# Row maxima of an attention kernel: five of twelve places per head pair take the queries' high part in row halves, 512 keys each

## The chip, the cores and the metric

The kernel is one program on one core of a Trainium2 chip. The metric is device time in microseconds, the median of several executions. The engines are TensorE (PE in the rows, its weight loads PEld), VectorE (DVE), ScalarE (ACT), GpSimd (POOL) and SyncE (SP), which issues most transfers.

## The reference

One layer on x of 8 sequences, 1024 tokens, width 256: causal attention with 16 heads over a latent of 64 numbers per token, a layer norm, a top-1 mixture of 32 experts with a capacity of 320 rows each, and a second layer norm.

```python
q = einsum('bld,dhk->blhk', x, Wq)
latent = einsum('bld,dc->blc', x, Wkv_down)
k = einsum('blc,chk->blhk', latent, Wk_up)
v = einsum('blc,chk->blhk', latent, Wv_up)
attn = softmax(where(mask, einsum('bqhd,bkhd->bhqk', q, k) / 8, -inf))
x = layernorm(x + einsum('bqhd,hdo->bqo', einsum('bhqk,bkhd->bqhd', attn, v), Wout))
x = layernorm(x + experts(x))        # router, capacity 320, silu(g) * u, gate
```

## The kernel before

The key and value matrices are folded into the query and output matrices, so that a head's query is 64 numbers wide and is multiplied with the latents directly. Queries and latents are split into a high and a low part, each in the rounded 32-bit type that TensorE multiplies in one pass. `q_hl[..][:, h, :]` holds 128 rows for head h: for head 0 the high part in rows 0 to 63 and the low part in rows 64 to 127, for head 1 the other way round. `lat_hi` holds the latents' high part twice, in both row halves. One matmul over 128 rows therefore multiplies a head's whole query with the latents' high part.

The main loop runs over 64 steps `gp` (8 sequences of 8 head pairs; p is the pair in its sequence) and 12 slots `t` in each, one for a block of 128 keys against 512 queries. The order on each engine is written out by hand:

- `turned_scores` (L742, L745) makes scores with keys on the partitions, for ScalarE's exponentials (L1011). The second matmul brings in the low latents and the row's maximum, which `q_max` holds as a 65th row.
- For that maximum the scores are made a second time, with queries on the partitions: `row_scores` (L717). Each call is a *unit*: a head, a block of 128 queries and up to 512 keys, into one of three PSUM banks in turn (`ROW_BANKS`). VectorE takes each unit's maximum in `row_max`: with the causal mask (L1175) where the unit ends on the diagonal, plainly (L1179) otherwise. A unit's matmul waits until the maximum of the unit three before it is done (`ROW_BEFORE`).
- `values` (L765) multiplies the exponentials with the latents, a head in each half of the array's columns, at even t for the two slots before the last two.

There are 24 units in a step, in pairs (both heads). `UNITS` lists them, and pair k is put at `PLACES[k]`: slot t, and 0 for right behind the slot's scores or 1 for the slot's end. The places (0, 0), (4, 0), (6, 0), (8, 0) and (10, 0), numbers 0, 4, 6, 8 and 10, stand right in front of value products. Step gp makes the units of step gp + 1, so 63 steps have them; step 0's own are made at the start. Widths of the pairs before, places 0 to 11: 128, 256, 384, 512, 320, 320, 512, 256, 512, 384, 512, 512 keys.

VectorE's order in slots 6 to 8 matters below: the two maxima of place 6, `copy_max` (L1190) of the transposed maxima that TensorE makes after the values (L727), `invert_rows` (L1209 four times, L1213), the two maxima of place 7, those of place 8, `invert_rows` again. Other matmul stages that follow a pair in some steps are `project_q` (L664), `turn_x` (L674), `turn_latents` (L690) and `total` (L777). L858 is a product of the setup.

Of the kernel before, what the change touches and what calls it, by code (L numbers as in the profile page):

```python
# [9 lines left out]
ACT = mybir.ActivationFunctionType  # L10
AX = mybir.AxisListType
F32 = mybir.dt.float32
# [4 lines left out]
P = 128  # L17
# [6 lines left out]
def build_layer(nc, x, Wq, Wkv, Wk_up, Wv_up, Wout, w_router, w_gate, w_up, w_down, out):  # L24
    B, L, D = x.shape
    _, H, HD = Wq.shape
    LD = Wkv.shape[1]
    E, _, F = w_gate.shape
    T = B * L
    C = int(math.ceil(1.25 * T / E))  # L30
    NT = L // P
# [3 lines left out]
    HPB = BANK // P  # L35
# [14 lines left out]
    first_query = lambda t: P * max(0, SLOT[t][1] - HPB * SLOT[t][0])  # L50
    on_diagonal = lambda t: SLOT[t][1] >= HPB * SLOT[t][0]

    UNITS = ([(h, i, 0) for i in range(HPB) for h in range(2)]
             + [(h, i, k) for i in range(HPB, NT) for k in range(2) for h in range(2)])
    NU = len(UNITS)

    unit_keys = lambda i, k: ((k * 5 * P // 2, (k + 1) * 5 * P // 2) if i == HPB
# [3 lines left out]
    PLACES = [(0, 0), (0, 1), (1, 1), (2, 1), (4, 0), (4, 1), (6, 0), (7, 0), (8, 0), (8, 1), (10, 0), (10, 1)]  # L61
# [4 lines left out]
    UNIT_ORDER = [(0, u) for u in range(2 * HPB)] + [unit for at in sorted(UNITS_AT) for unit in UNITS_AT[at]]  # L66
    UNIT = {unit: n for n, unit in enumerate(UNIT_ORDER)}
    assert len(UNIT) == PAIRS * NU == len(UNIT_ORDER)

    kept_by = lambda n: n // NSLOT * NT + sum(on_diagonal(t) for t in range(n % NSLOT + 1))  # L70
    NPROBS = 6
# [15 lines left out]
    with ExitStack() as ctx:  # L87
        def sb(name, shape, dt=F32, stack=ctx):
            return stack.enter_context(nc.sbuf_tensor(name, shape, dt))
# [10 lines left out]
        stat6 = sb("stat6", [P, 16, 6])  # L100
# [18 lines left out]
        lat_hi = [sb(f"lat_hi{i}", [P, L], F32R, attn) for i in range(2)]  # L119
        lat_lo = [sb(f"lat_lo{i}", [LD + 1, L], F32R, attn) for i in range(2)]  # L120
        lat_keys = [sb(f"lat_keys{i}", [P, NT, LD], F32, attn) for i in range(2)]
        q_hl = [sb(f"q_hl{i}", [P, 2, L], F32R, attn) for i in range(2)]
# [14 lines left out]
        x1 = sb("x1", [P, NT, W], F32, attn)  # L137
# [4 lines left out]
        alone = sb("alone", [P, 3, NT], F32, attn)  # L142
# [14 lines left out]
        x_in = [sb(f"x_in{i}", [P, NT, D], F32, attn) for i in range(2)]  # L157
# [17 lines left out]
        tail = ExitStack()  # L175
# [5 lines left out]
        NY = 5  # L181
# [1 line left out]
        ex_xT = sb("ex_xT", [P, 2, KD, 2 * C], F32, tail)  # L183
        ex_s = sb("ex_s", [P, 4, KF, C], F32, tail)
        ex_h = sb("ex_h", [P, 4, KF, C], F32, tail)
        ex_y = sb("ex_y", [P, 2, NY, D], F32, tail)
        neg_mean = sb("neg_mean", [P, 2 * NY], F32, tail)
        shift = sb("shift", [P, 2 * NY], F32, tail)
        tail.close()
# [61 lines left out]
        ex_sent = [sem(f"ex_sent{i}") for i in range(4)]  # L251
# [25 lines left out]
        for gp in range(PAIRS):  # L277
            b, p = divmod(gp, NPAIR)
# [85 lines left out]
        ex_ring = [row_ps[0], row_ps[1], value_ps, misc_ps]  # L364
# [5 lines left out]
        def _(sp):  # L370
# [23 lines left out]
            for gp in range(PAIRS):  # L394
                b, p = divmod(gp, NPAIR)
# [49 lines left out]
            sp.wait_ge(alone_stored, 16 * B)  # L445
            for e in range(AHEAD, E):
                g = (e - AHEAD) // 2
                sp.wait_ge(ex_sent[g % 2], 16 * NY * (g // 2 + 1))
                load_rows(e)
                load_weights(e)  # L450
            for k in range(2):
                sp.wait_ge(ex_sent[k], 16 * NY * (E // 4))

        @block.gpsimd
        def _(pool):
# [121 lines left out]
            for gp in range(PAIRS):  # L577
                b, p = divmod(gp, NPAIR)
# [42 lines left out]
            def send_back(g):  # L621
                pool.wait_ge(ex_o_ready, g + 1)
                for n in range(NY):
                    nc.gpsimd.indirect_dma_start(
                        out=out_rows, out_offset=bass.IndirectOffsetOnAxis(
                            ap=ex_x[:, g % (AHEAD // 2), n, TOKEN:W].bitcast(I32), axis=0),
                        in_=ex_y[:, g % 2, n, :], in_offset=None, bounds_check=T - 1, oob_is_err=False
                        ).then_inc(ex_sent[g % 2], 16)

            for g in range(E // 2):  # L630
                root(g)
# [3 lines left out]
        def _(pe):  # L635
# [67 lines left out]
            def row_scores(gp, u):  # L703

                h, i, k = UNITS[u]
                n = UNIT[gp, u]
                b = gp // NPAIR
                if u in (0, 2 * HPB):
                    wait_emptied(pe, ("q", gp, u // (2 * HPB)))
                    if gp % NPAIR == 0:  # L710
                        wait_emptied(pe, ("lat", b, u // (2 * HPB)))
                if n >= 2:
                    if n in ROW_BEFORE:
                        pe.wait_ge(max_done, ROW_BEFORE[n] + 1)
                k0, k1 = unit_keys(i, k)
                dst = ROW_BANKS[row_bank(n)]
                nc.tensor.matmul(dst[:, 0:k1 - k0], q_hl[gp % 2][:, h, i * P:(i + 1) * P], lat_hi[b % 2][:, k0:k1],  # L717
                                 start=True, stop=True).then_inc(rows_full, 1)

            def turn_max(gp, c):  # L720
# [119 lines left out]
            for c in range(4):  # L840
                bank = take(("wqT", c))
# [4 lines left out]
            bank = take(("wkT", 0))  # L846
# [6 lines left out]
            for kd in range(KD):  # L853
                banks = [take(("A", h, kd)) for h in range(2)]
                for j in range(NPAIR):
                    for h in range(2):
                        rows = slice(h * HD, (h + 1) * HD)
# [15 lines left out]
            bank = take(("wvT", 0))  # L873
# [4 lines left out]
            for c in range(4):  # L878
                banks = [take(("V", h, c)) for h in range(2)]
                for j in (2 * c, 2 * c + 1):  # L880
                    for h in range(2):
                        rows = slice(h * HD, (h + 1) * HD)
# [94 lines left out]
        def _(act):  # L977
# [50 lines left out]

            def pass_alone(b, i):

                act.wait_ge(x1_ready, b * 2 + i // HPB + 1)
                act.wait_ge(alone_scale, b * 2 + i // HPB + 1)
                ins = nc.scalar.activation(x_in[b % 2][:, i, :], x1[:, i, 0:D], ACT.Identity, scale=alone[:, 2, i:i + 1])
                if i == NT - 1:
                    ins.then_inc(alone_ready, 1)

# [9 lines left out]
            bank = wait_full(act, use)  # L1046
            nc.scalar.copy(wkT, bank).then_inc(free_of(use), 1)
            for kd in range(KD):
                for h in range(2):
                    bank = wait_full(act, ("A", h, kd))  # L1050
                    dst = fold_hi[:, kd, :].rearrange("p (j h c) -> p j h c", h=2, c=LD)[:, :, h, :]
# [46 lines left out]
            def normalise_out(g):  # L1098
                act.wait_ge(shift_ready, g + 1)
                for n in range(NY):  # L1100
                    k = g % 2 * NY + n
                    last = nc.scalar.activation(ex_y[:, g % 2, n, :], ex_y[:, g % 2, n, :], ACT.Identity,
                                                bias=shift[:, k:k + 1], scale=rstd[:, k:k + 1])
                last.then_inc(ex_o_ready, 1)

# [8 lines left out]
        def _(dve):  # L1114
# [265 lines left out]
            def add_to_rows(g):  # L1380

                part = slice(g % 2 * NY, (g % 2 + 1) * NY)
                if g >= 2:
                    dve.wait_ge(ex_sent[g % 2], 16 * NY * (g // 2))
                for n in range(NY):
                    bank, _ = y_use(g, n)
                    row = ex_x[:, g % (AHEAD // 2), n, :]
                    dve.wait_ge(ex_y_full, g * NY + n + 1)
                    nc.vector.scalar_tensor_tensor(ex_y[:, g % 2, n, :], ex_ring[2 + bank][:, 0:D],
                                                   row[:, GATE:TOKEN], row[:, 0:D], ALU.mult, ALU.add  # L1390
                                                   ).then_inc(ex_y_free[bank], 1)
                for n in range(NY):
                    bank, uses = y_use(g, n)
                    dve.wait_ge(ex_y_free[bank], uses + 1)
                    last = nc.vector.bn_stats(stat6[:, g % 2 * NY + n, :], ex_y[:, g % 2, n, :])
                step(last)
                settle()
                for n in range(NY):
                    last = nc.vector.bn_aggr(mean_var[:, g % 2 * NY + n, :], stat6[:, g % 2 * NY + n, :])
                last.then_inc(var_ready, 1)  # L1400
# [30 lines left out]
```

## Time and profile before

| | |
|---|---|
| median of 3 runs | 2441.88 us (2440.73 to 2442.39) |
| profiled execution, its own time | 2441.89 us |
| its span on the core | 2440.1 us |
| mean granted TensorE clock | 0.974 |
| TensorE matmuls busy | 2319.8 us, 95% |
| weight loads busy | 1509.0 us, 62% |
| VectorE | 1517.1 us, 62% |
| ScalarE | 1041.7 us, 43% |
| GpSimd | 1715.3 us, 70% |
| row units' matmuls (L717) | 1536, 512 keys in 640 of them |

The page gives each engine's busy time and the chain that ended last. The timeline gives the start and the length of single instructions. Matmuls are pipelined: a matmul of 512 columns is shown 0.40 us long, but the next starts 0.24 us after it. So what a matmul costs is read from start to start, not from its length. A line with "x2" merges two instructions in a row. Where two lines merge, the time in front covers both.

### The profile page before, as it was taken

How to read it: one execution, taken by the hardware profiler on the slowest of the kernel's cores; microseconds unless marked ns; L12 is line 12 of the kernel's file. 1: busy time of each engine (PE TensorE's matmuls, PEld its weight loads, DVE VectorE, ACT ScalarE, POOL GpSimd, SP SyncE). 2: the span in 40 equal slices, each digit the busy share in tenths (PEclk: the TensorE clock that was granted, in tenths of full speed). 3: DMA queues.
4: the chain of work that ended last, by engine and by line, in shares of the span. 5: the costliest groups of instructions: out<-in, count | busy, mean ns of one | idle time of the engine just before them, and what ended most of it. 6: DMA issues, size and time to landing. Idle time of an engine off the chain costs nothing.

```text
span 2440.1 us, 36843 instructions
## 1 busy us (share of the span) xinstructions
PE 2319.8 (95%) x11528; PEld 1509.0 (62%) x11528; DVE 1517.1 (62%) x4450; ACT 1041.7 (43%) x2048; POOL 1715.3 (70%) x1774
## 2 busy tenths in 40 slices
PE   6999999999999999999999999999999999849996
PEld 5565576556655666567655765566656665537774
DVE  4677656765576657765776567656766577225553
ACT  3454435543455445443544354534554454112222
POOL 0688767986788667975797669867886679524444
PEclk8999999999999999999999999999999999969998
DMA  3222200200011001100020002100110011234552
GB/s 89 62 65 62 62 10 19 65 24 18 14 44 49 14 14 36 53 19 14 19 73 21 10 19 61 27 18 14 44 49 14 14 33 41 67 110 150 183 184 67
DMA packets 96819, 118.97 MB, mean 49 GB/s; under 512 B 12288, under 2 KB 75782, under 8 KB 96624
## 3 DMA queue, kind: packets, MB, share of 16 engines
q1 hardware_dynamic: 89712, 99.98, 14.9%
q0 software_dynamic: 6912, 16.64, 2.0%
q8 instruction: 93, 1.52, 0.3%
q14 instruction: 102, 0.84, 0.1%
HBM read 46.91 MB, written 37.90 MB: 35 GB/s over the span
## 4 chain that ended last, share of the span: by engine, by line
PE 83%; DVE 7%; issue 4%; POOL 3%; ACT 2%; DMA 0%; SPq 0%; DVEq 0%; POOLq 0%; ACTq 0%
PE value_ps L765 20%; PE misc_ps L787 9%; PE turned_ps L742 9%; PE turned_ps L745 9%; PE misc_ps L664 8%; PE row_ps L717 7%; PE turned_ps L938 6%; PE turned_ps L717 3%; PE misc_ps L777 2%; DVE rinv L1209 1%; PE value_ps L957 1%; PE misc_ps L957 1%; POOL half_sums L516 1%; DVE masked_row L1175 1%; PE misc_ps L813 1%
## 5 line engine op out<-in xcount | busy, mean ns | idle before, releaser
L1011 ACT ACTIVATE probs<-turned_ps 128x512 f32<-128x512 f32 (+2 forms) x1280 | 647.7, 555 | 779.6 <-PE turned_ps L745 749.1
L516 POOL TENSOR_TENSOR half_sums<-half_sums,probs 128x1024 f32<-128x1024 f32 (+3 forms) x512 | 832.2, 1625 | 30.0 <-ACT probs L1011 14.1
L765 PE MATMUL value_ps<-probs,lat_keys 128*64 128x512 f32 (+3 forms) x3072 | 589.1, 505 | 2.2 <-POOL probs L491 2.2
L742 PE MATMUL turned_ps<-q_hl,lat_hi 128*128 128x512 f32 (+2 forms) x1280 | 500.2, 393 | 1.5 <-ACT fold_v L1064 1.5
L745 PE MATMUL turned_ps<-q_max,lat_lo 65*128 65x512 f32 (+2 forms) x1280 | 480.4, 375 | 1.8 <-DMA q_max<-both_rows 1.8
L491 POOL TENSOR_SCALAR_AFFINE_SELECT probs<-probs 128x256 f32<-128x256 f32 x512 | 210.6, 411 | 354.6 <-ACT probs L1011 352.0
L1175 DVE CUSTOM_DVE_ANT_0 masked_row<-row_ps,future 128x512 bf16<-128x512 f32 (+4 forms) x707 | 344.7, 508 | 136.5 <-PE row_ps L717 130.4
L765 PEld LDWEIGHTS value_ps<-probs,lat_keys 128*64 128x64 f32 x3072 | 188.2, 137 | 278.0 <-issue 211.6
L511 POOL TENSOR_TENSOR half_sums<-probs 128x768 f32<-128x768 f32 (+1 forms) x128 | 269.6, 2106 | 118.7 <-ACT probs L1011 118.6
L717 PE MATMUL row_ps<-lat_hi,q_hl 128*128 128x512 f32 (+4 forms) x1026 | 340.6, 373 | 4.9 <-DVE neg_max L1175 4.0
L717 PEld LDWEIGHTS row_ps<-lat_hi,q_hl 128*128 128x128 f32 x1026 | 189.6, 191 | 150.7 <-issue 69.7
L742 PEld LDWEIGHTS turned_ps<-q_hl,lat_hi 128*128 128x128 f32 x1280 | 243.3, 190 | 39.2 <-ACT probs L1011 10.0
L745 PEld LDWEIGHTS turned_ps<-q_max,lat_lo 65*128 65x128 f32 x1280 | 244.2, 191 | 27.7 <-DMA q_max<-both_rows 2.3
L1179 DVE TENSOR_REDUCE unit_max<-row_ps 128x1 f32<-128x512 f32 (+1 forms) x319 | 199.9, 643 | 77.0 <-PE row_ps L717 77.0
L787 PE MATMUL misc_ps<-fold_v,headsT 128*128 128x256 f32 x1008 | 232.5, 383 | 6.3 <-DVE x L1237 3.6
L787 PEld LDWEIGHTS misc_ps<-fold_v,headsT 128*128 128x128 f32 x1008 | 187.6, 190 | 47.4 <-issue 13.9
L717 PE MATMUL turned_ps<-lat_hi,q_hl 128*128 128x320 f32 x510 | 182.4, 358 | 6.5 <-DVE unit_max L1175 2.7
L523 POOL TENSOR_TENSOR headsT<-headsT,rinv_rows 128x512 f32<-128x512 f32 x128 | 165.4, 1292 | 22.7 <-DVE rinv_rows L1213 22.7
L991 ACT CAST q_hl<-misc_ps 64x512 fp32r<-64x512 f32 x125 | 72.6, 581 | 216.6 <-PE misc_ps L664 216.6
L1175 DVE CUSTOM_DVE_ANT_0 masked_row<-turned_ps,future 128x256 bf16<-128x256 f32 (+1 forms) x317 | 160.6, 507 | 3.4 <-PE turned_ps L717 1.5
L938 PE MATMUL turned_ps<-ex_xT,ex_w 128*128 128x320 f32 x512 | 145.6, 438 | 0.0
L1237 DVE TENSOR_TENSOR x<-misc_ps,x_in 128x256 f32<-128x256 f32 x64 | 27.2, 425 | 186.7 <-PE misc_ps L787 186.7
(195 smaller groups left out, 2728.2 us busy)
## 6 DMA issues: line engine op xcount, KB each, us to landing
q_max<-q_hl SPq DMA_DIRECT2D x256, 128.0 KB
slots_x<-router SPq DMA_DIRECT2D x8, 1290.0 KB, 5.9
ex_x<-slots_x SPq DMA_DIRECT2D x64, 129.0 KB, 2.3
x_in<-in_L_attn_x_bld SPq DMA_DIRECT2D x8, 1024.0 KB, 5.6
layer_out<-x_in SPq DMA_DIRECT2D x8, 1024.0 KB, 4.5
ex_w<-in_L_ffn_w_gate SPq DMA_DIRECT2D x32, 256.0 KB, 3.7
ex_w<-in_L_ffn_w_up SPq DMA_DIRECT2D x32, 256.0 KB, 3.8
ex_w<-in_L_ffn_w_down SPq DMA_DIRECT2D x32, 256.0 KB, 4.4
```

The costliest lines, as they stand in the source:

```text
L491: nc.gpsimd.affine_select(out=block, in_=block, pattern=[[0, 2], [1, P]], compare_op=ALU.is_ge, fill=0.0, base=0, channel_multiplier=-1).t ...
L511: nc.gpsimd.tensor_tensor(sums_of(gp, c)[:, :, q0:BANK], before[:, :, q0:BANK], now[:, :, q0:BANK], ALU.add).then_inc(added, 1)
L516: nc.gpsimd.tensor_tensor(total, total, now[:, :, q0:BANK], ALU.add).then_inc(added, 1)
L717: nc.tensor.matmul(dst[:, 0:k1 - k0], q_hl[gp % 2][:, h, i * P:(i + 1) * P], lat_hi[b % 2][:, k0:k1], start=True, stop=True).then_inc(rows ...
L742: nc.tensor.matmul(scores_of(n, h), lat_hi[b % 2][:, keys], q_hl[gp % 2][:, heads, cols], start=True, stop=False)
L745: nc.tensor.matmul(scores_of(n, h), lat_lo[b % 2][:, keys], q_max[:, c, heads, q0:BANK], start=False, stop=True).then_inc(turned_full, 1)
L765: mm = nc.tensor.matmul(value_ps[h * LD:(h + 1) * LD, q0:BANK], lat_keys[b % 2][:, j, :], probs[:, n % NPROBS, h, q0:BANK], start=(j == 0) ...
L787: mm = nc.tensor.matmul(bank[:, 0:D], headsT[:, (NPAIR * b + j) % NHEADS, i * P:(i + 1) * P], fold_v[:, j, :], start=(j == 0), stop=(j == ...
L938: mm = nc.tensor.matmul(turned_ps[f][:, m, 0:C], ex_w[e % AHEAD][:, m, kd, f * P:(f + 1) * P], ex_xT[:, g % 2, kd, u * C:(u + 1) * C], sta ...
L1011: nc.scalar.activation(probs[:, n % NPROBS, heads, q0:BANK], scores_of(n, h), ACT.Exp).then_inc(exp_done, 1)
L1175: nc.vector.tensor_tensor_reduce(masked_row[n % 2][:, 0:width], row[:, 0:width], future[:, BANK - width:], scale=-1.0, scalar=-MASKED, op0 ...
L1179: nc.vector.tensor_reduce(dst, row[:, 0:width], AX.X, ALU.max, negate=True).then_inc(max_done, 1)
```

## The change

`UNITS` has another order. Widths of the pairs are now 512, 128, 256, 384, 512, 320, 512, 320, 512, 256, 512, 384 keys for places 0 to 11: the same units, but all five places in front of value products now have 512 keys. In those five places a unit's matmul takes only the 64 rows of its own head's high part (`rows_of`): rows 0 to 63 for head 0, rows 64 to 127 for head 1. The queries' low part is left out of these maxima; they only shift the exponent, and the sums are made with the same shift. Step 0's own units keep 128 rows. The rest of the diff gives names to sizes (`NOUT = 2`, `x_out`) and changes no instruction.

```diff
-    UNITS = ([(h, i, 0) for i in range(HPB) for h in range(2)]
-             + [(h, i, k) for i in range(HPB, NT) for k in range(2) for h in range(2)])
+    UNITS = [(h, i, k) for i, k in ((3, 0), (0, 0), (1, 0), (2, 0), (5, 0), (4, 0), (6, 0), (4, 1), (7, 0), (5, 1), (7, 1), (6, 1))
+             for h in range(2)]
...
+    IN_ROW_HALVES = [k for k, (t, end) in enumerate(PLACES) if t % 2 == 0 and not end]
+    rows_of = lambda gp, u, h: slice(h * LD, (h + 1) * LD) if gp and u // 2 in IN_ROW_HALVES else slice(0, P)
...
-                nc.tensor.matmul(dst[:, 0:k1 - k0], q_hl[gp % 2][:, h, i * P:(i + 1) * P], lat_hi[b % 2][:, k0:k1],
+                rows = rows_of(gp, u, h)
+                nc.tensor.matmul(dst[:, 0:k1 - k0], q_hl[gp % 2][rows, h, i * P:(i + 1) * P], lat_hi[b % 2][rows, k0:k1],
                                  start=True, stop=True).then_inc(rows_full, 1)
```

## Rows read from the trace of the kernel before

**Rows 1.** Page, part 4: the chain that ended last, by engine.
```profile
PE 83%; DVE 7%; issue 4%; POOL 3%; ACT 2%; DMA 0%; SPq 0%; DVEq 0%; POOLq 0%; ACTq 0%
```
**Rows 2.** Windows, one step: length, then each engine's busy time, clock, DMA.
```profile
100.65:127.63 26.98, 26.83 (x136) 16.11 (x134) 19.55 (x59) 13.40 (x27) 22.86 (x22) 1.00 0.24 69
```
**Rows 3.** Timeline of a pair of 512 before values, and a pair after them.
```profile
1002.86 0.40 PE L745 MATMUL turned_ps<-q_max,lat_lo 65*128 65x512 f32 x1
...
1003.33 0.40 PE L717 MATMUL row_ps<-lat_hi,q_hl 128*128 128x512 f32 x1
1003.66 0.20 PEld L765 LDWEIGHTS value_ps<-probs,lat_keys 128*64 128x64 f32 x4 [0.37 <-ACT probs L1011]
...
1005.53 0.50 PE L717 MATMUL row_ps<-lat_hi,q_hl 128*128 128x512 f32 x1
1005.63 0.19 PEld L717 LDWEIGHTS turned_ps<-lat_hi,q_hl 128*128 128x128 f32 x1
1005.86 0.39 PE L717 MATMUL turned_ps<-lat_hi,q_hl 128*128 128x512 f32 x1
```
**Rows 4.** Timeline: a load of 64 rows behind a matmul over the full array.
```profile
533.25 0.40 PE L745 MATMUL turned_ps<-q_max,lat_lo 65*128 65x512 f32 x1
...
533.58 0.57 PEld L690 LDWEIGHTS misc_ps<-ident,x1T 64*128 64x128 f32 x8 [0.37 <-issue]
```
**Rows 5.** Setup product in row halves: first loads; all loads (min/median/max ns); window.
```profile
19.41 0.32 PEld L858 LDWEIGHTS turned_ps<-headsT 64*128 64x128 f32 x2 [1.45 <-ACT headsT L1047]
...
L858 PEld LDWEIGHTS turned_ps<-headsT x64: 282/330/330, 19.4 to 26.0; 64*128 64x128 f32 x64
...
19.50:26.10 6.60, 6.60 (x63) 6.60 (x64) 1.29 (x2) 1.09 (x2) 0.00 (x0) 0.50 0.01 2
```
**Rows 6.** Timeline: last score matmul and first value product around places 0, 4, 4.
```profile
92.58 0.39 PE L745 MATMUL turned_ps<-q_max,lat_lo 65*128 65x512 f32 x1
...
93.08 1.73 PE L765 MATMUL value_ps<-probs,lat_keys 128*64 128x512 f32 x8
...
100.41 0.40 PE L745 MATMUL turned_ps<-q_max,lat_lo 65*128 65x512 f32 x1
...
101.14 0.65 PE L765 MATMUL value_ps<-probs,lat_keys 128*64 128x512 f32 x2
...
236.24 0.39 PE L745 MATMUL turned_ps<-q_max,lat_lo 65*128 65x512 f32 x1
...
236.85 1.08 PE L765 MATMUL value_ps<-probs,lat_keys 128*64 128x512 f32 x4
```
**Rows 7.** Timeline, places 6 to 8: VectorE's chain and the load that waits for it.
```profile
106.60 1.29 DVE L1179 TENSOR_REDUCE unit_max<-row_ps 128x1 f32<-128x512 f32 x2 [1.15 <-PE row_ps L717]
...
107.52 0.27 PE L727 MATMUL misc_ps<-ident,neg_max 128*8 128x128 f32 x1
...
107.90 0.28 DVE L1190 CAST both_rows<-misc_ps 8x128 fp32r<-8x128 f32 x1
...
110.29 0.19 PEld L717 LDWEIGHTS turned_ps<-lat_hi,q_hl 128*128 128x128 f32 x1 [0.58 <-DVE unit_max L1175]
...
2064.89 0.19 PEld L717 LDWEIGHTS turned_ps<-lat_hi,q_hl 128*128 128x128 f32 x1 [0.58 <-DVE unit_max L1175]
```
**Rows 8.** Groups by form: one masked maximum of 256 and of 320 keys.
```profile
L1175 DVE CUSTOM_DVE_ANT_0 masked_row<-turned_ps,future 128x256 bf16<-128x256 f32 x126 | 50.8, 403 | 2.7 <-PE turned_ps L717 0.7 <-issue 0.2
...
L1175 DVE CUSTOM_DVE_ANT_0 masked_row<-turned_ps,future 128x320 bf16<-128x320 f32 x64 | 31.1, 486 | 0.0
```
**Rows 9.** Timeline: place 10 of a step with p = 6.
```profile
252.58 0.40 PE L745 MATMUL turned_ps<-q_max,lat_lo 65*128 65x512 f32 x1
...
253.53 1.94 PE L765 MATMUL value_ps<-probs,lat_keys 128*64 128x512 f32 x8
```
**Rows 10.** Timeline: a unit of 256 keys and the matmul behind it.
```profile
108.68 0.29 PE L717 MATMUL row_ps<-lat_hi,q_hl 128*128 128x256 f32 x1
108.81 0.40 PE L742 MATMUL turned_ps<-q_hl,lat_hi 128*128 128x512 f32 x1
```

More of the change, by code:

```diff
@@ L185, in build_layer @@
         ex_h = sb("ex_h", [P, 4, KF, C], F32, tail)
-        ex_y = sb("ex_y", [P, 2, NY, D], F32, tail)
+        NOUT = 2
+        ex_y = sb("ex_y", [P, NOUT, NY, D], F32, tail)
         neg_mean = sb("neg_mean", [P, 2 * NY], F32, tail)
@@ L447, in _ @@
                 g = (e - AHEAD) // 2
-                sp.wait_ge(ex_sent[g % 2], 16 * NY * (g // 2 + 1))
+                sp.wait_ge(ex_sent[g % NOUT], 16 * NY * (g // NOUT + 1))
                 load_rows(e)
                 load_weights(e)
-            for k in range(2):
-                sp.wait_ge(ex_sent[k], 16 * NY * (E // 4))
+            for k in range(NOUT):
+                sp.wait_ge(ex_sent[k], 16 * NY * (E // 2 // NOUT))
         @block.gpsimd
@@ L626, in send_back @@
                             ap=ex_x[:, g % (AHEAD // 2), n, TOKEN:W].bitcast(I32), axis=0),
-                        in_=ex_y[:, g % 2, n, :], in_offset=None, bounds_check=T - 1, oob_is_err=False
-                        ).then_inc(ex_sent[g % 2], 16)
+                        in_=ex_y[:, g % NOUT, n, :], in_offset=None, bounds_check=T - 1, oob_is_err=False
+                        ).then_inc(ex_sent[g % NOUT], 16)
             for g in range(E // 2):
@@ L1029, in pass_alone @@
             def pass_alone(b, i):
+                x_out = x_in[b % 2]
                 act.wait_ge(x1_ready, b * 2 + i // HPB + 1)
                 act.wait_ge(alone_scale, b * 2 + i // HPB + 1)
-                ins = nc.scalar.activation(x_in[b % 2][:, i, :], x1[:, i, 0:D], ACT.Identity, scale=alone[:, 2, i:i + 1])
+                ins = nc.scalar.activation(x_out[:, i, :], x1[:, i, 0:D], ACT.Identity, scale=alone[:, 2, i:i + 1])
                 if i == NT - 1:
@@ L1101, in normalise_out @@
                     k = g % 2 * NY + n
-                    last = nc.scalar.activation(ex_y[:, g % 2, n, :], ex_y[:, g % 2, n, :], ACT.Identity,
+                    last = nc.scalar.activation(ex_y[:, g % NOUT, n, :], ex_y[:, g % NOUT, n, :], ACT.Identity,
                                                 bias=shift[:, k:k + 1], scale=rstd[:, k:k + 1])
@@ L1382, in add_to_rows @@
                 part = slice(g % 2 * NY, (g % 2 + 1) * NY)
-                if g >= 2:
-                    dve.wait_ge(ex_sent[g % 2], 16 * NY * (g // 2))
+                if g >= NOUT:
+                    dve.wait_ge(ex_sent[g % NOUT], 16 * NY * (g // NOUT))
                 for n in range(NY):
@@ L1388, in add_to_rows @@
                     dve.wait_ge(ex_y_full, g * NY + n + 1)
-                    nc.vector.scalar_tensor_tensor(ex_y[:, g % 2, n, :], ex_ring[2 + bank][:, 0:D],
+                    nc.vector.scalar_tensor_tensor(ex_y[:, g % NOUT, n, :], ex_ring[2 + bank][:, 0:D],
                                                    row[:, GATE:TOKEN], row[:, 0:D], ALU.mult, ALU.add
@@ L1394, in add_to_rows @@
                     dve.wait_ge(ex_y_free[bank], uses + 1)
-                    last = nc.vector.bn_stats(stat6[:, g % 2 * NY + n, :], ex_y[:, g % 2, n, :])
+                    last = nc.vector.bn_stats(stat6[:, g % 2 * NY + n, :], ex_y[:, g % NOUT, n, :])
                 step(last)
```

## The prediction

> **What bounds the kernel now.** I read the chain first: 83% of what ended last is TensorE, 7% VectorE [rows 1]. One step shows the same: in 26.98 us TensorE's matmuls cover 26.83, VectorE works 19.6 and GpSimd 22.9 [rows 2]. GpSimd has 4 us to spare in a step, so no change of some tenths makes it the bound. What counts is when matmuls start, so the rest is read from the timeline, start to start. There a pair of 512 keys at place 10 stands like this [rows 3]: last score matmul at 1002.86, the second unit two matmuls later at 1003.33, first load of the values at 1003.66. A matmul of 512 costs 0.235 while the array goes on in the same shape. The last step is 0.33, that is 0.095 more: values use column halves, and their load is not started under the running matmul, it waits until the array is empty. After the values it is the same, and the unit's own load is open too: first unit at 1005.53, second load let in at 1005.63, second unit at 1005.86. So an open load is 0.107 (0.33 less the 0.23 of a unit). Pairs in front of values have the emptying behind them already.
>
> **A pair in row halves.** The diff hopes that the two units run side by side. The question is what stands in front of them: the array goes from 128 rows to 64. That step is in the trace [rows 4]: a load of 64 rows and 128 columns behind the same L745 starts 0.33 after it (533.25 to 533.58), in all seven steps that have one (0.318 to 0.330). So changing the row shape empties the array as changing the column shape does. I price the new pair from the last score matmul on: 0.33 until the loads start, 0.107 for the open load, then 0.23 and 0.095 until the values' load: 0.762. That holds if the second head's load and matmul go beside the first's. Row halves are in the trace once, in a setup product [rows 5]: the first two loads cover 0.32 together, where the shortest of the 64 takes 0.282, so the second starts 0.04 after the first at most; all 64 fit in about 6.6 us at the granted clock of 0.5 (1.2 GHz), a pair in 0.21. So loads lie side by side. For the matmuls the rows are weaker: 0.21 for a pair of them would also hold two in a row of 64 columns and two passes each (half of the 0.21 at that clock). I take side by side, and 0.77 for the pair: the bounds are 0.762 and 0.80 (the full 0.04 added). The bound from the other side, matmuls in a row, is 1.00.
>
> The Trainium skill, TensorEngine Tiling (Array Packing), Theoretical Speedup, says that a contraction of at most 64 gives up to twice the rate; by that alone 315 pairs (5 in each of 63 steps) would each save one unit of 0.235, 74 us in all, for 2368. The same page, Key Properties, says that a change of the tiling mode drains TensorE, and the trace agrees with this one (0.33 against 0.235).
>
> **The five places.** Before, a pair costs, from last score matmul to values: place 0 (128 keys) 0.50; place 4 (320) 0.73 where the second load waits for VectorE, 0.61 where not (p = 1, 2, 6); places 6, 8, 10 (512) 0.80 [rows 3, 6]. After, each is 0.77. So place 0 is +0.27, place 4 +0.04 (+0.15 or so for p = 1, 2, 6), the others -0.025 each. Place 4's wait goes, as place 3 now has 384 keys for VectorE instead of 512.
>
> **The other seven.** 128 keys are worth 0.058 on a matmul: 512 cost 0.235, 256 cost 0.12 [rows 3, 10]. Places 2, 3, 9 and 11 lose 128 keys in both units: 4 x 0.115 = -0.46. Place 1 goes from 256 to 128, but there a load (0.107) is longer than the matmul, so only -0.03. Place 7 goes from 256 to 320: +0.06. Together -0.43.
>
> **Where TensorE runs free** a step's sum is 0.27 + 0.04 - 0.075 - 0.43 = -0.195, or -0.085 with the dearer place 4.
>
> **The wait at place 8.** In 27 of the 63 steps (p = 4, 5, 7, those with p = 1 to 3 of the first sequence, and the last) the second unit of place 8 waits for VectorE; its load comes at 110.29 in the first of them, at 2064.89 in the last, with 0.58 idle before [rows 7]. Its bank is freed by the first maximum of place 7, and VectorE reaches that by a chain that starts with place 6: two maxima from 106.60, the copy at 107.90, four reciprocals, a transpose, the mask. What happens to the chain's start? Before, the first unit of place 6 starts 0.235 after the last score matmul and VectorE follows 0.43 behind. Now both units really start at 0.437, so VectorE begins 0.20 later, though the pair as a whole is done earlier. Of this 0.095 is absorbed: the copy at 107.90 waits for TensorE's L727 (107.52, it always comes 0.38 later), and could follow the maxima 0.095 sooner, as it does in the steps where VectorE is late. That leaves 0.105, and the mask of 320 keys instead of 256 adds 0.07 (486 against 403 ns [rows 8], a little less from start to start). So the load at place 8 comes 0.18 later than now, and nothing that TensorE saved at places 6 or 8 helps. A step with this wait: 0.27 + 0.04 - 0.025 (place 10) + 0.18 (places 6 to 8 with place 7) - 0.49 (places 1, 2, 3, 9, 11) = -0.025. Behind the waiting load stand the values of slot 8 and everything after them on TensorE; VectorE has 0.8 us idle before place 9, so the delay is not passed on twice.
>
> In steps with p = 6 VectorE is late already at place 6, so the later start costs nothing; there place 10 takes 0.95 (252.58 to 253.53) instead of 0.80 [rows 9] because it waits for place 9's masks, which shrink from 384 to 256 keys: -0.145 more, so -0.23. In steps with p = 3 the spare time before place 8 is 0.08 and shrinks to some 0.03: still free. For p = 0, 1, 2 other work stands in slot 7 and the spare time is above 0.4.
>
> **The sum.** 14 steps (p = 0, 3) x -0.195 = -2.7; 14 (p = 1, 2) x -0.085 = -1.2; 7 (p = 6) x -0.23 = -1.6; 27 x -0.025 = -0.7. Step 0 and the setup units have the same units in another order, behind VectorE there: 0, give or take 0.5. In all -6.2 us on the profiled execution's 2441.89 (span 2440.1 and 1.8 around it; the runs' median is 2441.88, the same): 2435.7, say 2436. VectorE, ScalarE and GpSimd have the same instructions; no DMA is added or moved, and SyncE's queue is untouched. The maxima of places 0 to 3 are done before TensorE transposes them in slot 6 as before.
>
> The largest unknown is the pair's 0.77. Some 256 pairs count with their length (not those of places 6 and 8 in the waiting steps): down to 0.762 is -2 us, up to 0.80 is +8. The chain's 0.18 may be 0.10 to 0.27 (nothing or everything absorbed): -2 to +2.5, and p = 3 and 6 could join with 0.15 each: +2. That gives 2431 to 2448.
>
> **Rivals.** *The loads are hidden*: if the emptying and the open load don't come, a pair costs 0.565, 0.205 less, 315 times: -65, so about 2371. The step of [rows 4] and the other six like it speak against it. Chance 5%. *The gain is eaten*: the second head trails by the full 0.04 and the chain passes all of its delay on: 2441.9 - 6.2 + 8 + 2.5 = 2446; with half of this 2441. What speaks for it is the 0.04 of [rows 5], though taken at the lower clock. This and the upper half of my own case fall within 0.2%, or 4.9 us, which is about what a measurement of this kernel can tell from no change. Chance of that band 30%. *Slower, because the halves take turns*: at each of the 315 pairs the second matmul starts only when the first is through. The second load then lies under the first matmul, so the price is 0.23, against 0.235 saved; with the emptying and the open load left over, +0.23 x 315 = +72, so about 2508. If only the loads take turns it is 0.107 x 315 = +34, so about 2470. It decides from 0.02 per pair, where the free steps' gain is gone. The setup product's loads [rows 5] speak against it for the loads, and say little on the matmuls; the four loads of column halves within 0.20 [rows 3] are the next nearest. Chance 10% for both together; 3% more for a granted clock that falls to its lower level in more stretches, as half of the array rests in ten matmuls of a step; and 4% for smaller delays above 2447.
>
> **Chances.** My case, 2431 to 2437: 48%. Faster by over 0.2% is 53% with the hidden loads; within 0.2% 30%; slower 17%. The range that leaves 2 in 10 out takes in the first two cases and not their far ends: 2427 to 2448. Most of what lies outside is above it.
>
> **What would show it.** In the changed kernel's timeline: from L745 to the units' loads 0.33 (right) or 0.24 (hidden loads); the two loads of a pair within 0.04, and the pair from score matmul to values 0.77; place 8's wait in the same 27 steps with its load 0.18 later after place 6; no wait at places 4 and 10. It is wrong if the pair takes over 0.80 (taking turns: about 1.00), if the wait at place 8 spreads to the steps with p = 0 or 2, or if the granted clock has more low stretches.

## The result

The changed kernel takes 2450.91 us (2449.33 to 2452.29, five executions) where the kernel before takes 2441.88 beside it. The ratio is 1.0040, with a 95% interval of 1.0026 to 1.0055. The change is slower by 9 us; the forecast was 2436.0, faster by 6. The profiled execution took 2450.91 us too, its span is 2449.2 us, 9.1 more than before, and the mean granted clock 0.971 for 0.974.

The page of the changed kernel, parts 1 and 4 (the second line answers [rows 1]):

```profile
PE 2323.4 (95%) x11528; PEld 1444.4 (59%) x11528; DVE 1516.3 (62%) x4450; ACT 1040.6 (42%) x2048; POOL 1712.0 (70%) x1774
...
PE 82%; DVE 6%; issue 4%; POOL 4%; ACT 3%; DMA 1%; SPq 0%; POOLq 0%; DVEq 0%; ACTq 0%
```

Weight loads lost 65 us of busy time and no other engine moved by more than 4. The shares of the chain can't tell 9 us. As in the forecast, the readings come from the timeline, start to start. The step that [rows 2] showed, in the same kind of window:

```profile
100.50:127.50 27.00, 26.90 (x136) 15.22 (x134) 19.52 (x59) 13.37 (x27) 22.81 (x22) 1.00 0.24 69
```

It takes as long as before, 27.00 and 26.98 us. The forecast for such a step, one with the wait at place 8, was 0.025 less.

**The pair is as forecast.** Timeline of the changed kernel at place 10 of the step of [rows 3], which stood there with 0.80 us from score matmul to values:

```profile
1005.61 0.39 PE L751 MATMUL turned_ps<-q_max,lat_lo 65*128 65x512 f32 x1
...
1005.93 0.49 PE L723 MATMUL turned_ps<-lat_hi,q_hl 64*128 64x512 f32 x1
1005.94 0.50 PE L723 MATMUL row_ps<-lat_hi,q_hl 64*128 64x512 f32 x1
1006.37 1.94 PE L771 MATMUL value_ps<-probs,lat_keys 128*64 128x512 f32 x8
...
1005.93 0.18 PEld L723 LDWEIGHTS turned_ps<-lat_hi,q_hl 64*128 64x128 f32 x1 [0.35 <-DVE unit_max L1182]
1005.94 0.18 PEld L723 LDWEIGHTS row_ps<-lat_hi,q_hl 64*128 64x128 f32 x1
```

0.32 to the first load, the second head 3 to 4 ns behind it, 0.43 to the values: 0.755 in all, just under the 0.762 to 0.80 of the forecast. The two heads do run side by side. They start 3 to 5 ns apart in 232 of the 315 pairs; in the other 83, nearly all at places 4, 8 and 10, the second unit's bank is not free yet.

**At place 4 TensorE still waits for a mask of place 3.** The stretch answers the second of [rows 6], which had 0.73 there; 0.77 was forecast, and it is 0.88:

```profile
98.23 0.68 DVE L1162 TENSOR_TENSOR q_hl<-misc_ps,q_hl 64x512 fp32r<-64x512 f32 x1 [0.31 <-ACT q_hl L998]
98.42 0.62 PE L723 MATMUL row_ps<-lat_hi,q_hl 128*128 128x384 f32 x2
...
98.93 0.69 DVE L1163 TENSOR_TENSOR q_hl<-misc_ps,q_hl 64x512 fp32r<-64x512 f32 x1
...
99.65 0.56 DVE L1182 CUSTOM_DVE_ANT_0 masked_row<-row_ps,future 128x384 bf16<-128x384 f32 x1
99.82 0.39 PE L751 MATMUL turned_ps<-q_max,lat_lo 65*128 65x512 f32 x1
...
100.14 0.49 PE L723 MATMUL turned_ps<-lat_hi,q_hl 64*128 64x512 f32 x1
100.27 0.50 PE L723 MATMUL row_ps<-lat_hi,q_hl 64*128 64x512 f32 x1
100.70 1.08 PE L771 MATMUL value_ps<-probs,lat_keys 128*64 128x512 f32 x4
```

The second unit starts 0.13 after the first, not 3 ns. Its bank is freed by the first mask of place 3. That mask is shorter now, but it starts at 99.65, behind the two subtractions that make the queries' low part (L1162, L1163), and those wait for ScalarE's copies. TensorE comes to place 4 earlier by what place 3 saved, and finds VectorE where it was.

**The stage bank is waited for more.** `misc_ps` is one PSUM bank that all stages but scores, units and values share. Waits of TensorE's loads, from before and then from the changed kernel: engine, tile and line, what was waited for, then total us, times, longest:

```profile
PEld misc_ps L664 <- DVE q_hl L1156: 11.8, 7, 1.7
...
PEld misc_ps L787 <- DVE x L1237: 6.0, 7, 1.0
...
PEld misc_ps L674 <- DVE q_hl L1156: 2.8, 7, 0.4
```

```profile
PEld misc_ps L669 <- DVE q_hl L1163: 12.8, 7, 1.8
...
PEld misc_ps L793 <- DVE x L1244: 8.8, 20, 1.0
...
PEld misc_ps L679 <- DVE q_hl L1163: 4.2, 7, 0.6
```

The stage behind `q_hl` in slot 3 waits 0.2 longer in each of its seven steps (2.8 to 4.2; for p = 1 and 2 other stages, L787 and L805, stand there and grow alike), and the bank that holds a projection until VectorE has added it (L1237, now L1244) is waited for 20 times instead of 7. The row of before that carries the first one was on the page of waits when I made the forecast; I did not ask what the shorter units would do to it.

**In steps with p = 3, place 11 waits too.** The second unit of place 11 takes the bank that the first maximum of place 10 frees, and VectorE comes to that maximum late, behind the low part of the queries and the tile count. The load in the fourth sequence, from before and then changed:

```profile
951.78 0.19 PEld L717 LDWEIGHTS turned_ps<-lat_hi,q_hl 128*128 128x128 f32 x1 [0.34 <-DVE unit_max L1179]
```

```profile
954.36 0.19 PEld L723 LDWEIGHTS turned_ps<-lat_hi,q_hl 128*128 128x128 f32 x1 [0.46 <-DVE unit_max L1182]
```

Slot 10 is 0.15 to 0.17 shorter for p = 0, 1 and 2; for p = 3 it is 0.01 longer.

**The changed kernel's step, class by class.** Starts of the same matmul in both traces, compared slot by slot (median of the sequences after the first, us):

| steps | forecast | measured | of it given back |
|---|---|---|---|
| 27 with the wait at place 8 | -0.025 | +0.024 | place 4 +0.15 for +0.04 |
| p = 0, 7 | -0.195 | +0.012 | place 4; slots 9 and 11 +0.06, +0.11 |
| p = 3, 7, its first slot left out | -0.195 | near 0 | place 4; slot 10 +0.16 |
| p = 1, 7 | -0.085 | +0.225 | slot 3 +0.20; slots 9 and 11 +0.06, +0.11 |
| p = 2, 7 | -0.085 | +0.095 | slot 3 +0.20; slot 11 +0.12 |
| p = 6, 7 | -0.230 | +0.381 | slot 3 +0.20; slots 9 and 11 +0.10, +0.11 |

In slots 9 and 11 it is not always the same wait: the stage bank for p = 0 and 1, ScalarE's copy of `x1T` in front of the routing product for p = 2, the next sequence's `xT_lo` and `lat_lo` from VectorE for p = 6.

27 x 0.024 + 7 x (0.012 + 0.225 + 0.095 + 0.381) = 5.6, where the forecast had -4.8 for these and -1.4 for p = 3.

**Most of the rest is clock.** Of the remaining 3.5 us some 2.5 lie in the first slot of the steps with p = 3 and the slot before it, and 1.2 in the experts' tail, where the clock is at 0.5 for 3.4 us more twice (start and step 0 are 0.6 shorter). In front of a step with p = 3 TensorE does the routing product of 32 small matmuls (L813, now L819), here as a piece of the changed kernel's chain (start, us):

```profile
922.10 3.76 PE misc_ps L819 x32
```

Windows over the first slot of such a step in the fourth and the fifth sequence, before and then changed (length, engines' busy times, granted clock, DMA):

```profile
923.17:928.07 4.90, 4.90 (x20) 2.42 (x19) 3.62 (x11) 1.59 (x3) 2.60 (x3) 0.65 0.00 0
1182.72:1187.62 4.90, 4.90 (x20) 2.48 (x19) 3.64 (x11) 1.59 (x3) 2.51 (x3) 0.65 0.01 3
```

```profile
925.70:930.80 5.10, 5.10 (x20) 1.89 (x19) 4.42 (x11) 1.48 (x3) 2.82 (x4) 0.67 0.00 0
1186.07:1192.20 6.13, 6.13 (x20) 2.48 (x19) 4.11 (x12) 1.59 (x3) 2.64 (x4) 0.53 0.01 3
```

The second is 1.0 us longer than the first in the changed kernel, with the same work: the clock stood at 0.5 (1.2 GHz) for longer. By the trace's record of the clock, one kernel below (late_before_not_p3) has all three cases: from the start of the slot before a step with p = 3 to the step's end it takes 32.3 us with nothing at 0.5, 33.15 with 3.4 us of it and 34.75 with 6.8. So the two sorts cost 0.9 and 2.45 there, and these two prices are used below for the other kernels too. Before, the seven steps have 0, 6.8, 3.4, 3.4, 3.4, 3.4 and 6.8 us; changed 3.4, 6.8, 3.4, 6.8, 3.4, 6.8 and 3.4. By the prices that is 8.5 and 11.0 us: the 2.5.

### The profile page after: what moved, and what is told of

Read it like the earlier page. It is cut to its first block, busy times and chain, and to the rows that moved or that the text cites. A ratio compares the mean times of both kernels' runs of the same rounds, so it can differ in the third digit from the quotient of the medians.

```text
span 2449.2 us, 36843 instructions
## 1 busy us (share of the span) xinstructions
PE 2323.4 (95%) x11528; PEld 1444.4 (59%) x11528; DVE 1516.3 (62%) x4450; ACT 1040.6 (42%) x2048; POOL 1712.0 (70%) x1774
## 3 DMA queue, kind: packets, MB, share of 16 engines
q1 hardware_dynamic: 89712, 99.98, 14.8%
## 4 chain that ended last, share of the span: by engine, by line
PE 82%; DVE 6%; issue 4%; POOL 4%; ACT 3%; DMA 1%; SPq 0%; POOLq 0%; DVEq 0%; ACTq 0%
PE value_ps L771 19%; PE misc_ps L793 9%; PE turned_ps L748 9%; PE turned_ps L751 9%; PE misc_ps L669 8%; PE row_ps L723 7%; PE turned_ps L944 6%; PE turned_ps L723 4%; PE misc_ps L783 2%; POOL half_sums L521 2%; PE misc_ps L963 1%; PE value_ps L963 1%; DVE q_hl L1163 1%; PE misc_ps L819 1%; DVE rinv L1216 1%
## 5 line engine op out<-in xcount | busy, mean ns | idle before, releaser
L1182 DVE CUSTOM_DVE_ANT_0 masked_row<-row_ps,future 128x512 bf16<-128x512 f32 (+4 forms) x707 | 354.3, 522 | 157.1 <-PE row_ps L723 144.3
L723 PE MATMUL row_ps<-lat_hi,q_hl 64*128 64x512 f32 (+5 forms) x1026 | 342.3, 416 | 4.7 <-DVE neg_max L1182 3.4
L723 PEld LDWEIGHTS row_ps<-lat_hi,q_hl 128*128 128x128 f32 (+1 forms) x1026 | 163.2, 188 | 192.1 <-issue 128.5
L1186 DVE TENSOR_REDUCE unit_max<-row_ps 128x1 f32<-128x320 f32 (+1 forms) x319 | 198.1, 638 | 91.4 <-PE row_ps L723 72.7
L723 PE MATMUL turned_ps<-lat_hi,q_hl 64*128 64x512 f32 (+1 forms) x510 | 194.8, 382 | 6.1 <-DVE unit_max L1182 1.6
L1182 DVE CUSTOM_DVE_ANT_0 masked_row<-turned_ps,future 128x512 bf16<-128x512 f32 (+1 forms) x317 | 152.6, 481 | 9.0 <-PE row_ps L723 2.9
L1244 DVE TENSOR_TENSOR x<-misc_ps,x_in 128x256 f32<-128x256 f32 x64 | 27.2, 424 | 188.9 <-PE misc_ps L793 188.9
```

The lines of the kernel that those rows point to most:

```text
L723: nc.tensor.matmul(dst[:, 0:k1 - k0], q_hl[gp % 2][rows, h, i * P:(i + 1) * P], lat_hi[b % 2][rows, k0:k1], start=True, stop=True).then_in ...
L1182: nc.vector.tensor_tensor_reduce(masked_row[n % 2][:, 0:width], row[:, 0:width], future[:, BANK - width:], scale=-1.0, scalar=-MASKED, op0 ...
L1186: nc.vector.tensor_reduce(dst, row[:, 0:width], AX.X, ALU.max, negate=True).then_inc(max_done, 1)
```

## The experiments

| kernel | us, median (range, executions) | ratio to before [95%] |
|---|---|---|
| order_only | 2460.61 (2454.95 to 2462.14, 5) | 1.0080 [1.0067, 1.0094] |
| halves_only | 2446.11 (2439.90 to 2447.88, 11) | 1.0018 [1.0009, 1.0027] |
| wide3 | 2450.82 (2447.61 to 2452.55, 4) | 1.0042 [1.0026, 1.0057] |
| wide9 | 2460.40 (2457.40 to 2461.19, 4) | 1.0077 [1.0062, 1.0093] |
| late_before | 2437.39 (2435.84 to 2438.80, 11) | 0.9983 [0.9974, 0.9992] |
| late_after | 2436.60 (2434.38 to 2441.70, 11) | 0.9983 [0.9974, 0.9992] |
| halves_8_10 | 2438.95 (2436.72 to 2440.86, 11) | 0.9993 [0.9984, 1.0002] |
| late_halves_6_8_10 | 2427.72 (2426.65 to 2428.10, 5) | 0.9945 [0.9931, 0.9958] |
| late_before_not_p3 | 2429.20 (2426.42 to 2431.94, 5) | 0.9951 [0.9937, 0.9964] |
| late_halves_6_8_10_not_p3 | 2427.51 (2423.98 to 2428.14, 5) | 0.9939 [0.9925, 0.9952] |
| after_again | 2451.41 (2449.98 to 2455.01, 5) | 1.0044 [1.0028, 1.0059] |
| last_again | 2427.52 (2425.40 to 2428.36, 3) | 0.9938 [0.9916, 0.9961] |

**One part alone.** The change has two parts, a new order and row halves. order_only has the order:

```diff
-    rows_of = lambda gp, u, h: slice(h * LD, (h + 1) * LD) if gp and u // 2 in IN_ROW_HALVES else slice(0, P)
+    rows_of = lambda gp, u, h: slice(h * LD, (h + 1) * LD) if False else slice(0, P)
```

> The new order of units alone, all matmuls over 128 rows. Theory A: the five pairs in halves are themselves a small gain (0.755 us each against 0.80), and the loss comes from the order: the wide pair at place 0 costs 0.30, and what the narrower pairs at places 2, 3, 9 and 11 save is mostly waited away soon after. By A the order alone is slower than the change by about 0.045 at places 0, 6, 8 (where free) and 10, some 200 pairs, less 0.105 in the 27 steps where VectorE's chain from place 6 is then not delayed: 9 - 3 = +6, so about 2457 (2453 to 2462). Theory B: emptying the array for the halves is the loss (0.2 us in 315 pairs), and the order alone is even or a gain: 2441 or below.

2460.61. The order alone costs 19 us in the medians, 10 more than the change. Part of both numbers is clock: the profiled execution is the lowest of the five, 2454.95 at a mean granted clock of 0.972, and the three slower ones ran at 0.969 to 0.970. Slot by slot, class by class as in the table above, the order costs some 9 us in the profile and the change 6, so the halves give back some 3 to 4. It isn't the halves that make the kernel slow. halves_only has the old list of `UNITS` and row halves at the same five places:

> The five places in row halves, with the old order of units (128, 320, 512, 512, 512 keys there). Theory A, place by place: place 0 (128 keys) 0.59 instead of 0.50, place 4 +0.07 where free and 0 where it waits, places 6, 8, 10 -0.045 each where free, and +0.105 in the 27 steps where the later first unit of place 6 starts VectorE's chain 0.2 later. Sum +4: about 2446 (2443 to 2449), between the kernel before and the change. Theory B: all of the loss, 2450 or more.

2446.11, as expected; but its eleven executions run from 2439.90 at a granted clock of 0.977 to 2447.88 at 0.972, so the 5 us are the weaker reading. By the slots of its profile row halves under the old order cost 3.3 us, through place 0 (+0.08 in every step) and place 8. Its place 0, with 128 keys, takes 0.32 + 0.003 + 0.255 = 0.58 instead of the 0.50 of [rows 6]. At places 6 and 10 the halves bring 0.04 to 0.05 each. At place 8 a step of the 27 is 0.115 longer: VectorE's chain starts later there, as forecast. By the slots the price of both parts together (6) is less than the sum of the two (9 and 3), since the new order gives the halves their long pairs.

**Is the time that place 3 saves waited away?** wide3 is the changed kernel with 128 more columns in the matmuls of place 3, which nobody reads. TensorE loses there what the order had saved; VectorE has the same work.

```diff
+                more = P if gp and u // 2 in WIDER else 0
-                nc.tensor.matmul(dst[:, 0:k1 - k0], q_hl[gp % 2][rows, h, i * P:(i + 1) * P], lat_hi[b % 2][rows, k0:k1],
+                nc.tensor.matmul(dst[:, 0:k1 - k0 + more], q_hl[gp % 2][rows, h, i * P:(i + 1) * P], lat_hi[b % 2][rows, k0 - k0 // BANK * more:k1 + (1 - k0 // BANK) * more],
```

> The changed kernel, and the matmuls of place 3 stream 512 keys instead of the 384 that VectorE reads (128 columns more, 0.058 each, 0.116 a pair, 63 pairs: 7.3 us of matmul time). Theory A (the time that a narrower place 3 saves is waited away at place 4, in slot 3 or at the misc bank): costs 0 to 1.5 us, because the wait shrinks by as much; 2451 to 2453. Rival: TensorE's time there is on the path: +7.3, so 2458.

2450.82, the same as without (2450.91). Timeline of wide3 in the stretch that was shown above for the changed kernel:

```profile
99.98 0.73 PE L725 MATMUL row_ps<-lat_hi,q_hl 128*128 128x512 f32 x2
...
101.21 0.56 DVE L1184 CUSTOM_DVE_ANT_0 masked_row<-row_ps,future 128x384 bf16<-128x384 f32 x1
101.49 0.40 PE L753 MATMUL turned_ps<-q_max,lat_lo 65*128 65x512 f32 x1
...
101.82 0.50 PE L725 MATMUL turned_ps<-lat_hi,q_hl 64*128 64x512 f32 x1
101.83 0.50 PE L725 MATMUL row_ps<-lat_hi,q_hl 64*128 64x512 f32 x1
102.26 1.08 PE L773 MATMUL value_ps<-probs,lat_keys 128*64 128x512 f32 x4
```

From place 3's first unit to the values of place 4 it is 2.28 us here (99.98 to 102.26) and 2.28 in the changed kernel (98.42 to 100.70). The units of place 3 take 0.117 more, and the second unit of place 4 no longer waits (0.01 between the two). Over all steps the comparison says the same: +0.117 in slot 2, and -0.110 in slot 4 or, for p = 1, 2 and 6, -0.116 in slot 3, at the stage bank. Making TensorE's work shorter at place 3 is worth nothing, and counting it was the main error of the forecast. The slots show that, not the two medians alone: wide3's profile has 10 us less at a clock of 0.5 in front of the steps with p = 3 and a step 0 that is 3.2 us longer, which nearly cancel.

wide9 does the same at place 9 (`WIDER = [9]`). Its extra 128 keys stand in front, so VectorE reads as many columns as before but of other keys, and the maximum is another one; the work is the same.

> The same at place 9: its matmuls stream 384 keys instead of 256, again 0.116 a pair and 7.3 us in all. By the alignment of the two traces this saving is kept in the 27 steps with the wait at place 8 and in p = 2 and 3, and given back by half in p = 0, 1 and 6. Theory A: +0.116 x 41 + 0.058 x 21 = +6, so about 2457. If saved matmul time were waited away everywhere: 0 to 1.

2460.40, more than the 2457 expected. In slot 8 it is 0.117 longer per step, and 0.06 (p = 0, 1) or 0.10 (p = 6) comes back in slot 9. In the 27 steps and for p = 2 all of it stays. For p = 3, where I had expected the same, 0.11 comes back in slot 10: the load that waited 0.46 above waits 0.35.

```profile
958.69 0.19 PEld L725 LDWEIGHTS turned_ps<-lat_hi,q_hl 128*128 128x128 f32 x1 [0.35 <-DVE unit_max L1184]
```

So place 9's saving was real in most steps, some 5 us in all (27 + 7 steps x 0.117, 14 x 0.06, next to nothing for p = 3 and 6). Between 400 and 2000 us 44 us are at 0.5, for 34 in the changed kernel; by the two prices that is 4.6, and the two together make about the 9.5 between the medians.

**Is VectorE's chain at place 8 the price of the order of its own work?** `invert_rows` stands in slot 6, in front of the masks of place 7 that place 8 waits for [rows 7]. late_before is the kernel before with this one edit, late_after the changed kernel with it:

```diff
-                    if gp and t in (6, 8):
+                    if gp and t in (7, 8):
```

> The kernel before, with VectorE's first invert_rows of a step moved from slot 6 to slot 7, behind the two maxima of place 7 (four reciprocals and a transpose, 1.7 us, that stood in front of them). This takes the wait out of place 8. Theory A (VectorE's order, not its amount, makes the wait of 0.41 us in 27 steps): -0.41 x 27 = -11, so about 2430 (2429 to 2434), GpSimd's division by these rows comes 0.5 us later and has room. Rival: VectorE is simply full there, the wait moves to places 9 or 10 or to GpSimd: 2440 or more.

> The changed kernel with the same move. The wait at place 8 is 0.59 us there by its trace (1.346 from the last score matmul to the values where 0.755 is the free pair): Theory A: -0.59 x 27 - 1 (p = 6) = -17, so about 2434, and then nearly as fast as the kernel before with the move, as the change's own loss in the other places remains. Rival as above: 2449 or more.

2437.39 and 2436.60, both above what was expected (2429 to 2434, and 2434). The wait at place 8 is gone in all 27 steps, -0.41 to -0.44 in each (11.3 us), and -0.59 in each in the changed kernel (15.8). The masks start right after their matmul, and place 8's pair, score matmul to values, takes 0.79. Timeline of late_before:

```profile
109.24 0.28 PE L717 MATMUL turned_ps<-lat_hi,q_hl 128*128 128x256 f32 x1
...
109.56 0.42 DVE L1175 CUSTOM_DVE_ANT_0 masked_row<-turned_ps,future 128x256 bf16<-128x256 f32 x1 [0.70 <-PE turned_ps L717]
...
110.20 0.39 PE L745 MATMUL turned_ps<-q_max,lat_lo 65*128 65x512 f32 x1
...
110.43 0.40 PE L717 MATMUL row_ps<-lat_hi,q_hl 128*128 128x512 f32 x1
...
110.99 0.65 PE L765 MATMUL value_ps<-probs,lat_keys 128*64 128x512 f32 x2
```

But only 4 us came out of the 11. Most of the missing part has one place: slot 10 of the seven steps with p = 3 is 0.75 longer (0.57 in late_after), 5.2 us. The start and the experts' tail are some 2 us longer in the profile. Timeline of late_before there:

```profile
943.47 1.07 DVE L1209 RECIPROCAL rinv<-sums_cols 32x16 f32<-32x16 f32 x4
944.58 0.71 DVE L1213 STREAM_TRANSPOSE rinv_rows<-rinv 128x512 f32<-128x512 f32 x1
...
946.26 0.68 DVE L1155 TENSOR_TENSOR q_hl<-misc_ps,q_hl 64x512 fp32r<-64x512 f32 x1
...
947.68 0.59 DVE L1296 TENSOR_REDUCE in_tiles<-onehot 128x32 f32<-128x256 bf16 x1
...
948.54 0.69 DVE L1179 TENSOR_REDUCE unit_max<-turned_ps 128x1 f32<-128x512 f32 x1
...
949.28 0.19 PEld L717 LDWEIGHTS turned_ps<-lat_hi,q_hl 128*128 128x128 f32 x1 [1.00 <-DVE unit_max L1179]
```

From 942.76 on VectorE is hardly idle: reciprocals, transpose, masks, the low part of the queries and the tile count stand in one row, and TensorE's load, of the second unit of place 11, waits 1.00 for the maximum at their end. late_before_not_p3 takes the move out of these seven steps:

```diff
-                    if gp and t in (7, 8):
+                    if gp and t in (6 if b and p == 3 else 7, 8):
```

> The kernel before with VectorE's first reciprocals of a step moved from slot 6 to slot 7 as in late_before, but left in slot 6 in the seven steps with p = 3 of the later sequences. Theory: late_before lost 0.75 us at place 10 in each of those seven, because reciprocals, transpose, the queries' low parts of slot 9 and the tile count then stand in one row on VectorE in front of the maxima that place 10 waits for. Left in slot 6 there, the 7 x 0.75 = 5.2 us come back: 2437.4 - 5.2 = 2432 (2430 to 2435). Rival: the 0.75 comes from something else that moved (the low clock in front of these steps, or GpSimd's earlier copy), then the time stays at 2437.

2429.20, lower than the 2430 to 2435 forecast. Slot 10 is 0.751 shorter in each of the seven steps (5.3 us), and all others stand. The other 3 us lie with the clock as far as the profiles tell: 122 us of the span at 0.5, for 131 in late_before, of which the stretches around the steps with p = 3 make 2.2 by the two prices.

**The halves where they pay.** Of the five places, 6, 8 and 10 have pairs of 512 in the old order too. halves_8_10 has row halves at two of them, late_halves_6_8_10 at all three, with the moved reciprocals:

```diff
+    IN_ROW_HALVES = [6, 8, 10]
```

> Old order of units, row halves at places 8 and 10 only, no move. By the trace of all five in the old order, place 10 gives 0.045 in all steps but p = 3 and 6 and place 8 gives 0.045 in the steps without its wait, and nothing starts VectorE's chain later: -0.045 x 49 - 0.045 x 28 = -3.5, so about 2438 (2436 to 2440).

> Old order of units, row halves at places 6, 8 and 10 only (all 512 keys), and the same move. With the chain of place 6 gone a pair in halves is worth 0.045 us wherever it stands: -0.045 x 182 = -8 against the kernel before with the move, so about 2422 (2420 to 2427). If the gain of halves is only a shift of waits: same as the kernel before with the move.

2438.95 and 2427.72. The first is not to be told from no change. The second is faster than both kernels, if just above its 2420 to 2427. Against late_before its slots are shorter by 0.02 to 0.05 at each of the three places, but not slot 10 of the steps with p = 3 and 6, which wait for VectorE: some 6 us of its 10.

> The old order with row halves at places 6, 8 and 10 alone and the moved reciprocals, but these left in slot 6 in the seven steps with p = 3 of the later sequences. By the same theory 7 x 0.75 less than the 2427.7 of the kernel that moves them everywhere: 2422.5 (2420 to 2426). If the wait at place 10 has another cause: 2427.7.

2427.51: a miss. Slot 10 is shorter by 0.79 in all seven steps with p = 3, and the time stayed. Their first slots took it: at 0.5 they have 6.8, 6.8, 3.4, 6.8, 6.8, 3.4 and 0 us here, and 6.8, 0, 3.4, 0, 3.4, 6.8 and 0 in late_halves_6_8_10. By the two prices above that is 11.6 less 6.7, or 4.9, against 7 x 0.79 = 5.5 saved.

**Whose are the low stretches?** Two kernels ran again, unchanged.

> The changed kernel once more, unchanged, for its granted clock alone: in its first profile 34 us between 400 and 2000 us ran at 0.5, against 27 us in the kernel before, always around the first pair of a step with p = 3, and these stretches are the largest part of what its steps with p = 3 lost (3.4 us). Theory: the stretches fall anew in every execution, so here they lie in other sequences and sum to something between 20 and 45 us, and the executions scatter by 3 us with them. Rival: they belong to the program, then they lie in the same sequences with the same 34 us.

> The kernel with row halves at places 6, 8 and 10 and the reciprocals left in slot 6 for p = 3, unchanged, once more. Its first profile had 34 us at 0.5 between 400 and 2000 us, the same kernel without this exception 20.5, and it missed its forecast of 2422.5 by 5 us, though place 10 gave back 0.79 in each of the seven steps. Theory: the clock took it, anew in every execution: here 20 to 30 us at 0.5 and 2422 to 2428. Rival: the 34 us are the program's own, and the time is 2427.5 again with the same stretches.

For the steps with p = 3 the theory of chance fell both times, and the rival holds. after_again has the same seven stretches, 3.4, 6.8, 3.4, 6.8, 3.4, 6.8 and 3.4 us, and last_again those of its first profile, on another chip, with 2427.52 us again. The same two windows of after_again:

```profile
925.10:930.20 5.10, 5.10 (x20) 1.88 (x19) 4.43 (x11) 1.48 (x3) 2.80 (x4) 0.67 0.00 0
1185.50:1191.60 6.10, 6.10 (x19) 2.45 (x19) 4.10 (x11) 1.59 (x3) 2.63 (x4) 0.52 0.01 3
```

So in these two kernels the low stretches around p = 3 belong to the program. That is not so of all of them. The second profile of the changed kernel has other ones in the setup, and one of 3.4 us at 2087 us that the first lacks. And executions of one kernel differ: halves_only takes 2439.90 us at a granted clock of 0.977 and 2447.88 at 0.972, late_after 2434.38 at 0.976 and 2441.70 at 0.971. No profile shows where these differ. What in the program sets the stretches is open too: kernels that differ by some us in where the routing product comes have other ones, and no run here moves that product alone.

## Why the prediction was wrong

**Right: the pair.** The emptying (0.32), the open load, and both heads side by side gave 0.755 for 0.77. The rivals that let the halves take turns fell, and so did the hidden loads. The rule of the Trainium skill, TensorEngine Tiling (Array Packing), Key Properties, that a change of the tiling mode drains TensorE, is what these rows show; the rate up to twice as high that the page's Theoretical Speedup gives comes down to 0.755 for 0.80 in a pair of 512 keys, and to a loss, 0.58 for 0.50, in one of 128.

**Right: places 0, 6, 10 and 8.** Place 0 cost +0.256 (0.27 forecast), places 6 and 10 brought 0.03 to 0.05 (0.025). The wait at place 8 stands in the same steps; its load was forecast 0.18 later. The changed kernel's line that answers the load at 110.29 in [rows 7]:

```profile
110.01 0.18 PEld L723 LDWEIGHTS turned_ps<-lat_hi,q_hl 64*128 64x128 f32 x1 [0.42 <-DVE unit_max L1182]
```

From the last score matmul in front of place 6 it comes 4.52 later (105.49 to 110.01), before 4.36 (105.93 to 110.29): +0.16. Slots 6 to 8, place 9 among them, come out at +0.03 in such a step; +0.065 was forecast (0.18 less 0.115).

**Wrong: "The other seven", -0.43.** The savings of the seven are there: place 3 is 0.13 shorter, places 1 and 2 together 0.14, 9 and 11 0.1 each. I took them as lying on the path from start to end. But TensorE is paced by others at more points of a step than place 8: at place 4 by VectorE's first mask of place 3, in slot 3 of p = 1, 2 and 6 by the stage bank, in slots 9 and 11 of p = 0, 1, 2 and 6 by that bank, by VectorE or by ScalarE, and at place 11 of p = 3 by VectorE's maxima of place 10. What it saves ahead of such a point it waits there. Over all steps that is 4.1 us in slot 3, 4.7 in slots 9 and 11, 1.2 at place 11 of p = 3, and at place 4 4.5 more than forecast. wide3 puts place 3's saving back and loses nothing, which shows it for place 4 and slot 3; for the later points wide9 shows it with 0.06 to 0.11 of its 0.117 in 28 steps. I had asked this for place 8 and, for p = 6, place 10, and for no other place.

**Wrong: place 4, "+0.04, the wait goes".** I let the wait go because place 3's mask is shorter. Its length doesn't count; its start does, and that is fixed by ScalarE's copies and two subtractions of 0.7 each. The place costs +0.15. For p = 1, 2 and 6, where TensorE has already waited in slot 3, it is 0.75, close to the 0.77 forecast.

**Wrong: p = 6, -0.23.** It lost 0.38, the most of all. Place 10 did shrink from the 0.95 of [rows 9] to 0.82, though place 9's masks still hold it up for 0.08; but slots 3, 9 and 11 give back 0.4. "The later start costs nothing" did not hold either: place 8 takes 0.90 there for 0.86.

**Not in the sum: the clock.** I gave a lower clock 3% as a rival "as half of the array rests". It is about 3 of the 9 us, and not for that reason: order_only, with no halves, has 138 us at 0.5 in its profile, halves_only, with all five places in halves, has 129 like the kernel before, and the changed kernel has 142.

The rival *The gain is eaten* had the right picture, a gain that meets a wait, and 2446 as its time; but it looked for the price in a dearer pair and in more delay at place 8, and neither came.

## What to carry to other kernels

An engine that is 95% busy is not free to run ahead. Before a saving on it is counted, follow it forward to the next instruction that waits for another engine or shares a bank with one, and ask whether that release moves as well. Where it doesn't, the saving ends there (place 3 here, though not place 9 in most steps); and what sets a release is often when its instruction can start, not how long it is. Here the cheap gain was in VectorE's order (one line, 0.5% with the exception for p = 3), in front of the wait at place 8 that the trace shows in 27 of 63 steps.

## What the runs showed of the hardware

- Two matmuls in row halves start 3 to 4 ns apart and run side by side: a pair of 512 columns takes 0.43 from its loads to the next load, a single one on the full array 0.235 and 0.33 with the emptying.
- Going to 64 rows costs 0.32 to 0.33 from the last matmul over the full array to the load, whatever the width of the pair. So the halves lose at 128 columns (0.58 for 0.50) and win at 512 (0.755 for 0.80).
- The stretches at the granted clock of 0.5 around the steps with p = 3 came back in a second profile of the same kernel, place for place, for two kernels, and they change with the program. Two kernels with the same matmuls differ by up to 17 us of them (122 and 139), an estimated 5 us of time by the two prices above. Other low stretches differ between executions: eleven of halves_only range over 8 us, with a granted clock of 0.977 in the shortest and 0.972 in the longest. A comparison of two kernels that differ by 0.2% can be a comparison of these stretches.
